# Second cross-attention's weight folds: two heads at once on 64-row halves of TensorE, folds regrouped

## The chip, the cores and the metric

One core of one Trainium2 chip runs the whole computation, two sequences of 512 tokens with 128 features. The metric is the device time of one execution in microseconds: 346.1 us before the change, the median of three runs (345.12, 346.10 and 346.39). A profile is of one more execution.

## The reference, cut to what matters

Two layers, each a cross-attention over 154 context tokens and a feed-forward part. The change is about the second cross-attention (16 heads of 64):

```python
x = x + xattn0(layernorm(x), ctx)          # 8 heads of 4
x = x + self_attention(layernorm(x))       # 16 heads of 8, causal, rotary, conv before
x = x + moe(layernorm(x))                  # 4 experts
q = layernorm(x) @ Wq                      # second cross-attention, 16 heads of 64
k, v = split(ctx @ Wkv)
dots = einsum('bhnd,bhmd->bhnm', q, k) * 64 ** -0.5 - (1 - mask) * 1e6
x = x + einsum('bhnm,bhmd->bhnd', softmax(dots), v) @ Wout + bout
x = x + ffn1(x)                            # small units, one Win and one Wout
```

The context and the weights are known from the start. So the kernel folds them: for each head h it computes `kk[h] = Wq[h] @ k[h]^T` (128 features x 154 keys) and `vw[h] = v[h] @ Wout[h]` (154 keys x 128 features), and the attention itself is then `x @ kk[h]`, softmax, and a sum with `vw[h]`.

## The kernel before, in words

The program writes one instruction list per engine: `sp` (SyncE, which issues DMAs), `pool` (GpSimd), `dve` (VectorE), `act` (ScalarE) and `pe` (TensorE). Each engine works through its list in order. Everything between engines goes by semaphores: an instruction that waits holds up all that is behind it on its engine.

In time, the stages are: the first cross-attention (stage A, units of eight heads by 128 tokens), the self-attention of both sequences, the experts, the second cross-attention (stage C) and the last feed-forward part. The folds for stage C have nothing to wait for but their weights. They are laid into the gaps of earlier stages by a written list, `PREC`, of 50 jobs. Head pairs of one 128-column chunk c of the weights (c = 0 to 7) make a chunk:

- `k` c and `v` c: one full-height matmul each (context against a chunk of Wk or Wv), for two heads; 308 and 320 columns.
- `kk` h: one job per head, 308 columns. The two heads of a chunk lie in the two 64-row halves of `wqT`, so each head's keys are held in `kz` with zeros in the other half, and a matmul runs over all 128 rows.
- `vw` (g, b): the four heads of two chunks against a Wout laid out with zeros (`woutZ`), two matmuls of 256 columns for the first 128 keys. `vr` (g, b): the same for the last 26 keys, four matmuls with 32 output partitions.
- `xv` b: not a fold; the values of sequence b of the self-attention, four matmuls.

TensorE issues a job in `fold_C`, ScalarE copies its result from PSUM to SBUF in `copy_C`, both in the order of the list. A float32 matmul stands in the trace as two passes, each with a weight load; so a `k` or `kk` job is two matmul records. The PSUM bank of job n is n mod 3 for n < 32, and after that bank 4 or 7. A job waits until the last job on its bank has been copied, and for the `k` or `v` job that it reads.

Where the list runs: jobs 0 to 2 and 3 to 5 inside the last units of stage A (`F_UNIT`). Then `queries_keys(0)` (the queries and keys of sequence 0, eight passes of 512 columns). Then jobs 6 to 25, up to `F_LN`. Then `turn("b")` transposes the normalised sequence 1; ScalarE copies it with scale and bias to `HT` (line 1150) and VectorE convolves it (lines 821 to 825). Then jobs 26 to 29, `queries_keys(1)`, and jobs 30 and 31. At `F_LATE` = 32 the first scores begin: 20 steps m of `scores_for_maximum`, whose row maxima VectorE takes (`maximum`, line 872). TensorE may be up to three steps ahead of VectorE, as there are three pairs of banks. From m = 2 on, one job of the list (32 to 49) follows each step. During these steps GpSimd splits the queries and keys of sequence 1 (lines 575 to 585), and SyncE stores them (lines 470 and 472) and, behind these, the maxima of chunk 0 (line 464). After step 19 come the score steps s of the self-attention, each with a ring of further maxima (line 882).

GpSimd zeroes `woutZ` (line 536) and `kz` (line 548) ahead of its stage-A units. SyncE's load of Wout waits for the first of them.

Of the kernel before, what the change touches and what calls it, by code (L numbers as in the profile page):

```python
# [27 lines left out]
P = 128  # L28
# [3 lines left out]
KEYS = 154  # L32
# [61 lines left out]
def program(nc, t_in, out):  # L94
    ctx = ExitStack()
    with ctx:
# [71 lines left out]

        cw = sb("cw", [P, 7632])
# [7 lines left out]
        assert c.at <= 7632  # L177
        c = Carve(cw)
# [68 lines left out]

        F_UNIT = (3, 6, 9)
        F_QKV = (14,30)
        F_LN = 26  # L250
        F_LATE = 32
        F_VALUES = 42
        F_MAX = 45

        def prec_jobs():

            for c in range(HC // 2 + 1):
                if c < HC // 2:
                    yield "k", c, 2
                    yield "v", c, 1  # L260
                if c >= 1:
                    yield "kk", 2 * c - 2, 1
                    yield "kk", 2 * c - 1, 1
                if c in (2, 4):
                    for b in range(B):
                        yield "vw", (c // 2 - 1, b), 1
                        yield "vr", (c // 2 - 1, b), 1
            for g in (2, 3):
                for b in range(B):
                    yield "vw", (g, b), 1  # L270
                    yield "vr", (g, b), 1


        PREC = list(prec_jobs())

        def fold_bank(n):
            if n < F_LATE:
                return n % 3
            return 7 if n % 2 else 4

        for b in range(B):
            PREC.insert(F_QKV[b], ("xv", b, 1))
        N_PREC = sum(j[2] for j in PREC)


        ld_x = [sem(f"ld_x{b}") for b in range(B)]
# [57 lines left out]
        PER = {"A": 1, "C": 2}  # L344
        LN_BANK = 7
        R_AT, R_COLS = 64, (QT + 1) * E
        Q4_BANK = (2, 7)
# [3 lines left out]
        SHIFTS = {"A": 2, "C": 3}  # L351
        Z_OWN, Z_CTX, Z_EARLY, Z_WOUT, Z_SLOT, Z_ALL = 1, 2, 5, 6, 8, 15 + SLOTS

# [36 lines left out]
        def first_bank(m):  # L390
            return (0, 2, 5)[(m - M0) % 3]

# [5 lines left out]
        def ring_bank(k):  # L398
            return 5 + k % 2

# [10 lines left out]
        def slot_bank(b, part):  # L411
            return 6 if part else LN_BANK

# [6 lines left out]
        def _(sp):  # L420
# [81 lines left out]
        def _(pool):  # L502
# [635 lines left out]
        def _(act):  # L1138
# [49 lines left out]
            def copy_C(n0, n1):  # L1188

                for n in range(n0, n1):  # L1190
                    kind, i, _ = PREC[n]
                    act.wait_ge(preC_mm, n + 1)
                    bank = fold_bank(n)
                    if kind == "k":
                        if n == 0:
                            act.wait_ge(zeroed, Z_ALL)
                        for j in range(2):
                            r = slice(64 * j, 64 * j + 64)
                            copy(kz[r, i % 2, j, :], PS[r, bank, 0:B * KEYS], float(HDC) ** -0.5).then_inc(preC_act, 1)
                    elif kind == "v":  # L1200
                        copy(vT[:, i % 4, :], PS[:, bank, 0:B * KPAD]).then_inc(preC_act, 1)
                    elif kind == "kk":
                        copy(kkC[:, :, i * KEYS:(i + 1) * KEYS],
                             PS[:, bank, 0:B * KEYS].rearrange("p (b k) -> p b k", b=B)).then_inc(preC_act, 1)
                    elif kind == "vw":
                        g, b = i
                        copy(vwCm[:, b, 512 * g:512 * g + 512], PS[:, bank, :]).then_inc(preC_act, 1)
# [43 lines left out]

            copy_C(F_LN, F_VALUES)
            act.wait_ge(preC_act, sum(j[2] for j in PREC[:F_VALUES]))
            values(0)
            no_values(0)
            copy_C(F_VALUES, F_MAX)
            copy_maxima(0)
# [118 lines left out]
        def _(pe):  # L1376
# [135 lines left out]
            def fold_C(n0, n1):  # L1512

                done = [0]
                for kind, i, k in PREC:
                    done.append(done[-1] + k)
                for n in range(n0, n1):
                    kind, i, _ = PREC[n]
                    bank = fold_bank(n)
                    if n == 0:  # L1520
                        pe.wait_ge(ld_c, 80)
                        pe.wait_ge(unit_shift["A"], SHIFTS["A"] * NT)
                    if n == F_LATE:
                        pe.wait_ge(ln_T["b"], B)
                        pe.wait_ge(qkv_read, 4 * B)
                    elif 3 <= n < F_LATE:
                        pe.wait_ge(preC_act, done[n - 2])
                    elif n >= F_LATE + 2:
                        pe.wait_ge(preC_act, done[n - 1])

                    if n == F_MAX:
                        pe.wait_ge(m_copied, 1)
                    if kind == "kk":
                        pe.wait_ge(preC_act, done[1 + PREC.index(("k", i // 2, 2))])
                    elif kind in ("vw", "vr"):
                        pe.wait_ge(preC_act, done[1 + PREC.index(("v", 2 * i[0] + 1, 1))])
                    if kind == "k":
# [3 lines left out]
                    elif kind == "kk":  # L1541
                        q = mm(PS[:, bank, 0:B * KEYS], wqT[:, i // 2, :], kz[:, (i // 2) % 2, i % 2, :])
                    elif kind == "vw":
                        g, b = i
                        for c in range(2):
                            q = mm(PS[:, bank, 256 * c:256 * c + 256], vT[:, (2 * g + c) % 4, b * KPAD:b * KPAD + KM],
                                   woutZ[:, 2 * g + c])
                    elif kind == "vr":
                        g, b = i
                        for j in range(4):  # L1550
                            c = 2 * g + j // 2
                            q = mm(PS[32 * j:32 * j + 32, bank, 0:D], vT[:, c % 4, b * KPAD + KM:b * KPAD + KPAD],
                                   woutZ[:, c, j % 2, :])
# [49 lines left out]
            fold_C(F_QKV[1], F_LATE)  # L1603
            pe.wait_ge(preC_act, sum(j[2] for j in PREC[:F_LATE]))
            pe.wait_ge(qkv_read, 4 * B)
            pe.wait_ge(consts_ready, 2)
            def turn_maxima(c):

                pe.wait_ge(m_part, 3 * (c + 1))
                if c == 0:  # L1610
                    pe.wait_ge(preC_act, sum(j[2] for j in PREC[:F_MAX - 1]))
                elif c == 1:
# [397 lines left out]
```

## Time and profile before

| | before |
|---|---|
| three runs, median (lowest, highest) | 346.1 us (345.12, 346.39) |
| the profiled execution: its own time | 344.6 us |
| its span, first to last instruction | 342.7 us |
| TensorE busy in the span | 319.4 us (93%) |
| VectorE, ScalarE, GpSimd busy | 240.8, 216.5, 127.6 us |
| TensorE's granted clock | 1.000 of full speed |
| chain that ended last: TensorE, ScalarE, VectorE | 64%, 13%, 12% |

The span lies 1.9 us under the execution's own time, and that is 1.5 us under the median of the three runs. Busy time of TensorE counts modelled matmul ends. "PEld" rows are its weight loads. A line number of TensorE or of a ScalarE copy is that of a helper (1378 is `mm`, 1140 is `copy`, 1393 and 1695 are transposes), so such rows are told apart by their tensors: `cw` is the buffer that holds the weights of the folds and their `k` and `v` results.

### The profile page before, as it was taken

To read this page: it belongs to the slowest core of one execution; us is meant where nothing else is said; L and a number is where in the kernel's file an instruction comes from. 1 tells how busy PE (TensorE), PEld (TensorE's weight loads), DVE (VectorE), ACT (ScalarE), POOL (GpSimd) and SP (SyncE) were. 2 spreads that over 40 slices of the span, in tenths; PEclk is the share of its full clock that TensorE was granted. 3 is DMA by queue.
4 is the path that set the end of the run, shared out by engine and by line. 5 is a ranking of instruction groups with operands and counts; after the bars stand their busy time and mean duration, and the time that the engine had idled before them with its cause. 6 is when DMAs were issued, how large, how long until landed. Compare 5 with 4: busy or idle time off the path is not lost.

```text
span 342.7 us, 6887 instructions
## 1 busy us (share of the span) xinstructions
PE 319.4 (93%) x2398; PEld 228.1 (67%) x2398; DVE 240.8 (70%) x594; ACT 216.5 (63%) x641; POOL 127.6 (37%) x183
## 2 busy tenths in 40 slices
PE   7799989998999999999899998998999899999886
PEld 2348878664655444455544898995678687878675
DVE  4988875884776788777652463369787867888476
ACT  1388885374455756555468754754766676676995
POOL 3455563110731444310631260410695525545400
PEclk9999999999999999999999999999999999999999
DMA  7590000084852430073002003200200000000002
GB/s 209 187 282 7 2 0 2 10 273 137 237 187 70 118 95 1 3 288 83 4 18 71 2 23 91 59 0 1 55 17 17 0 2 0 4 0 0 2 0 63
DMA packets 21880, 22.47 MB, mean 66 GB/s; under 512 B 3894, under 2 KB 18646, under 8 KB 21846
## 3 DMA queue, kind: packets, MB, share of 16 engines
q1 hardware_dynamic: 18982, 16.78, 16.8%
q10 hardware_dynamic: 2352, 4.20, 3.6%
q0 software_dynamic: 512, 1.05, 1.0%
q8 instruction: 20, 0.33, 0.4%
q14 instruction: 14, 0.11, 0.1%
HBM read 14.22 MB, written 7.60 MB: 64 GB/s over the span
## 4 chain that ended last, share of the span: by engine, by line
PE 64%; ACT 13%; DVE 12%; issue 4%; POOL 4%; DMA 3%; ACTq 0%; POOLq 0%; DVEq 0%
PE PS L1378 57%; PE PS L1432 5%; ACT big L1166 5%; ACT big L1354 3%; POOL big L528 2%; DVE big L690 2%; DVE big L715 2%; DMA X<-in_x 1%; PE PS L1695 1%; DMA XN<-scr_y,pos 1%; DVE mB L882 1%; DVE stats L656 1%; DVE XN L667 1%; ACT big L1140 1%; POOL big L530 1%
## 5 line engine op out<-in xcount | busy, mean ns | idle before, releaser
L1378 PE MATMUL PS<-big 128*128 128x128 f32 (+10 forms) x592 | 95.6, 308 | 6.6 <-DVE mB L882 2.3
L1378 PEld LDWEIGHTS PS<-big 128*128 128x128 f32 (+3 forms) x592 | 58.3, 150 | 34.7 <-issue 11.3
L528 POOL TENSOR_TENSOR big<-big,urec 128x1024 f32<-128x1024 f32 x24 | 45.6, 1898 | 59.9 <-DVE urec L722 45.5
L1166 ACT ACTIVATE big<-big 128x154 f32<-128x154 f32 x192 | 60.5, 318 | 10.1 <-DVE big L690 5.0
L1296 ACT ACTIVATE big<-PS 128x1024 f32<-128x1024 f32 (+3 forms) x64 | 42.9, 702 | 30.2 <-PE PS L1378 30.1
L1140 ACT ACTIVATE big<-PS 128x1280 f32<-128x1280 f32 (+2 forms) x30 | 32.3, 1087 | 27.0 <-PE PS L1432 24.5
L882 DVE TENSOR_REDUCE mB<-PS 128x2 f32<-128x256 f32 (+2 forms) x66 | 38.6, 600 | 11.9 <-PE PS L1378 11.6
L1378 PE MATMUL PS<-kkC,XT 128*128 128x462 f32 (+1 forms) x96 | 36.0, 511 | 1.9 <-DVE big L715 1.9
L1378 PE MATMUL PS<-cstb 128*128 128x128 bf16 x192 | 37.5, 220 | 0.0
L516 POOL TENSOR_TENSOR rstd<-ve,minus_half 128x4 f32<-128x4 f32 (+2 forms) x13 | 13.2, 1016 | 63.4 <-DVE ve L662 63.4
L1166 ACT ACTIVATION_READ_ACCUMULATOR big<-big 128x1 f32 x192 | 36.1, 188 | 0.0
L1378 PEld LDWEIGHTS PS<-vwCm,big 128*128 128x128 f32 x256 | 30.9, 192 | 3.9 <-ACT big L1140 1.3
L1432 PE MATMUL PS<-cst,big 128*128 128x128 f32 x240 | 30.6, 275 | 2.4 <-POOL big L530 1.8
L1378 PE MATMUL PS<-vwCm,big 128*128 128x128 f32 x256 | 31.3, 276 | 1.0 <-DVE X L745 0.5
L704 DVE TENSOR_REDUCE mraw<-PS 128x3 f32<-128x462 f32 (+1 forms) x48 | 26.0, 579 | 7.2 <-PE PS L1378 5.8
L1432 PEld LDWEIGHTS PS<-cst,big 128*128 128x128 f32 x240 | 26.6, 141 | 6.4 <-POOL big L530 6.2
L715 DVE SCALAR_TENSOR_TENSOR big<-PS,rowbias,umax 128x462 f32<-128x462 f32 (+1 forms) x48 | 27.5, 629 | 0.0
L1378 PEld LDWEIGHTS PS<-kkC,XT 128*128 128x128 f32 x96 | 17.0, 190 | 15.0 <-issue 11.9
L1378 PE MATMUL PS<-big,cw 128*32 128x512 f32 (+3 forms) x256 | 23.8, 444 | 0.3
L1378 PE MATMUL PS<-cw 128*32 128x128 f32 (+2 forms) x128 | 22.5, 351 | 0.8 <-ACT vwCm L1140 0.7
L606 POOL TENSOR_SCALAR_AFFINE_SELECT big<-big 128x256 f32<-128x256 f32 x32 | 12.9, 408 | 24.2 <-ACT big L1296 23.9
L1378 PEld LDWEIGHTS PS<-cstb 128*128 128x128 bf16 x192 | 18.9, 98 | 3.2 <-issue 1.6
(191 smaller groups left out, 508.1 us busy)
## 6 DMA issues: line engine op xcount, KB each, us to landing
scr_qk<-big SPq DMA_DIRECT2D x12, 384.0 KB, 3.4
big<-scr_qk SPq DMA_DIRECT2D x16, 288.0 KB
big<-in_wv ACTq DMA_DIRECT2D x1, 2048.0 KB, 7.9
scr_x<-zrow SPq DMA_DIRECT2D x2, 448.0 KB, 7.0
scr_y<-big SPq DMA_DIRECT2D x2, 448.0 KB, 3.9
X<-in_x ACTq DMA_DIRECT2D x2, 256.0 KB, 4.0
big<-in_A_WoT ACTq DMA_DIRECT2D x1, 512.0 KB, 5.0
cw<-in_C_Wk SPq DMA_DIRECT2D x1, 512.0 KB, 4.7
```

The lines of the kernel that those rows point to most:

```text
L516: pool.tensor_tensor(rstd[:, s], ve[:, s], minus_half[:, s], ALU.pow).then_inc(ln_rstd[name], 1)
L528: pool.tensor_tensor(pn[:, 0:GH * P].rearrange("p (h k) -> p h k", h=GH), Pt[u % 3][:, :, 0:KM], r.to_broadcast([P, GH, KM]), ALU.mult).th ...
L606: pool.affine_select(PTb[:, slot:slot + 2, 0:P], PTb[:, slot:slot + 2, 0:P], [[0, 2], [1, P]], ALU.is_ge, 0.0, base=0, channel_multiplier= ...
L704: own(dve.tensor_reduce(mraw[:, u % 2, h0:h1], s, AX.X, ALU.max))
L715: dve.scalar_tensor_tensor(Pt[u % 3][:, h0:h1, :], s, bias(u), umax[:, u % 2, h0:h1].unsqueeze(2).to_broadcast([P, h1 - h0, KEYS]), ALU.ad ...
L882: dve.tensor_reduce(mB[:, b, h:h + len(heads), qt], PS[:, ring_bank(k), 0:len(heads) * w].rearrange("p (j w) -> p j w", w=w), AX.X, ALU.ma ...
L1140: return act.activation(dst, src, ACT.Copy, scale=scale)
L1166: i = act.activation(Pt[u % 3][:, h, :], Pt[u % 3][:, h, :], ACT.Exp, accum_out=usum[:, u % 3, h:h + 1])
L1296: act.activation(PTb[:, slot:slot + 2, 0:w], PS[:, 2 * pair:2 * pair + 2, 0:w], ACT.Exp, scale=float(HDB) ** -0.5).then_inc(st_exp, 1)
L1354: act.activation(RJ[:, j, c], sT[:, c], ACT.Relu, scale=vec[:, V_W1 + j:V_W1 + j + 1], bias=vec[:, V_B1 + j:V_B1 + j + 1]).then_inc(relu_r ...
L1378: return pe.matmul(o, lhsT, rhs, start=start, stop=stop)
L1432: i = pe.transpose(PS[:, T_BANK[st] + k // 4, (k % 4) * P:(k % 4) * P + P], PN[v % 2][:, k * P:k * P + P], ident)
```

## The change

The two heads of a chunk are multiplied as two matmuls of 64 rows each, one on rows 0 to 63 and one on rows 64 to 127, each into a bank of its own. `kz` and `woutZ` with their zeros and memsets are gone, `kT` and `wout` are plain. A `kk` job now covers two heads and a `vw` job writes two banks, and each is copied by one ScalarE instruction over both banks (616 columns for `kk`, 512 for `vw`). A `k` result is copied whole, in one instruction in place of two of 64 partitions. The list has 42 jobs. `fold_banks` gives each job one or two neighbouring banks, of 0 to 2 before `F_LATE` and of 6 and 7 after it, and the copy that it has to wait for.

The new places: jobs 0 to 2 and 3, 4 in stage A; 5 to 26 between `queries_keys(0)` and `turn("b")`; 27 to 32 before `queries_keys(1)`; 33 after it. Jobs 34 to 41 (four `vw`, four `vr`) follow the even steps m = 2 to 16. The maxima of chunk 0 are turned at m = 13.

The list with its banks, and behind the slash the job whose copy a job waits for:
`k0[0] v0[1] k1[2] | v1[0]/k0 kk0[1,2]/k1 | k2[0]/v1 v2[1]/kk0 kk1[0,1]/v2 vw00[0,1]/kk1 vr00[2] xv0[0]/vw00 vw01[1,2]/vr00 vr01[0]/xv0 k3[1]/vw01 v3[2]/vw01 kk2[0,1]/k3 k4[2]/v3 v4[0]/kk2 kk3[1,2]/k4 vw10[0,1]/kk3 vr10[2]/kk3 vw11[0,1]/vw10 vr11[2]/vr10 k5[0]/vw11 v5[1]/vw11 kk4[0,1]/v5 k6[2] | v6[0]/kk4 kk5[1,2]/k6 k7[0]/v6 v7[1]/kk5 kk6[0,1]/v7 kk7[0,1]/kk6 | xv1[2]/k7`; then in the score steps `vw20[6,7] vr20[6]/vw20 vw21[6,7]/vr20 vr21[6]/vw21` and the same for 30 and 31.

```diff
-        woutZ = c.f32(HC * D).rearrange("p (c j o) -> p c j o", c=8, j=2)
-        kz = c.f32(2 * 2 * B * KEYS).rearrange("p (r j n) -> p r j n", r=2, j=2)
+        wout = c.f32(HC * D // 2).rearrange("p (c o) -> p c o", c=8)
+        kT = c.f32(2 * B * KEYS).rearrange("p (r n) -> p r n", r=2)
...
-        F_UNIT = (3, 6, 9)
-        F_QKV = (14,30)
-        F_LN = 26
-        F_LATE = 32
-        F_VALUES = 42
-        F_MAX = 45
+        F_UNIT = (3, 5)
+        F_QKV = (10, 33)
+        F_LN = 27
+        F_LATE = 34
+        F_MAX = 40
+        M_FOLDS = range(2, 18, 2)
+        M_CHUNK0 = 13
...
+        def fold_banks():
+            used, at = {}, 0
+            for n, (kind, _) in enumerate(PREC):
+                ring = (0, 1, 2) if n < F_LATE else (6, 7)
+                if n == F_LATE:
+                    at = 0
+                pair = kind in ("kk", "vw")
+                if pair and at % len(ring) == len(ring) - 1:
+                    at += 1
+                banks = [ring[(at + j) % len(ring)] for j in range(1 + pair)]
+                at += len(banks)
+                FOLD_BANKS.append(banks)
+                FOLD_AFTER.append(max(used.get(k, 0) for k in banks))
+                for k in banks:
+                    used[k] = n + 1
...
-        AV_BANK = 4
-        GROUP_BANK = ((7, 7, 7, 7), (6, 5, 6, 5))
+        AV_BANK = 6
+        GROUP_BANK = ((7, 7, 7, 7), (4, 5, 4, 5))
...
-            sp.wait_ge(zeroed, Z_WOUT)
-            for j in range(2):
-                sp.dma_start(woutZ[64 * j:64 * j + 64, :, j, :],
-                             i["C_Wout"].rearrange("(c j e) o -> j e c o", j=2, e=HDC)[j]).then_inc(ld_c, 16)
+            sp.dma_start(wout, i["C_Wout"].rearrange("(c p) o -> p c o", p=P)).then_inc(ld_c, 16)
...
-            pool.memset(woutZ, 0.0).then_inc(zeroed, 1)
-            pool.memset(kz, 0.0).then_inc(zeroed, 1)
...
                     if kind == "k":
-                        for j in range(2):
-                            r = slice(64 * j, 64 * j + 64)
-                            copy(kz[r, i % 2, j, :], PS[r, bank, 0:B * KEYS], float(HDC) ** -0.5).then_inc(preC_act, 1)
+                        copy(kT[:, i % 2, :], PS[:, bank, 0:B * KEYS], float(HDC) ** -0.5).then_inc(preC_act, 1)
...
                     elif kind == "kk":
-                        copy(kkC[:, :, i * KEYS:(i + 1) * KEYS],
-                             PS[:, bank, 0:B * KEYS].rearrange("p (b k) -> p b k", b=B)).then_inc(preC_act, 1)
+                        copy(kkC[:, :, 2 * i * KEYS:(2 * i + 2) * KEYS].rearrange("p b (j k) -> p j b k", j=2),
+                             fold_out(n, B * KEYS).rearrange("p j (b k) -> p j b k", b=B)).then_inc(preC_act, 1)
...
+                    after = FOLD_AFTER[n]
                     if kind == "kk":
-                        pe.wait_ge(preC_act, done[1 + PREC.index(("k", i // 2, 2))])
+                        after = max(after, 1 + PREC.index(("k", i)))
...
+                    if after:
+                        pe.wait_ge(preC_act, after)
...
                     elif kind == "kk":
-                        q = mm(PS[:, bank, 0:B * KEYS], wqT[:, i // 2, :], kz[:, (i // 2) % 2, i % 2, :])
+                        for j, half in enumerate(HALVES):
+                            q = mm(PS[:, FOLD_BANKS[n][j], 0:B * KEYS], wqT[half, i, :], kT[half, i % 2, :])
                     elif kind == "vw":
                         g, b = i
                         for c in range(2):
-                            q = mm(PS[:, bank, 256 * c:256 * c + 256], vT[:, (2 * g + c) % 4, b * KPAD:b * KPAD + KM],
-                                   woutZ[:, 2 * g + c])
+                            for j, half in enumerate(HALVES):
+                                q = mm(PS[:, FOLD_BANKS[n][j], c * D:c * D + D],
+                                       vT[half, (2 * g + c) % 4, b * KPAD:b * KPAD + KM], wout[half, 2 * g + c, :])
...
-                if m >= 2 and late < len(PREC):
+                if m in M_FOLDS:
                     fold_C(late, late + 1)
                     late += 1
-                if late == F_MAX:
+                if m == M_CHUNK0:
                     turn_maxima(0)
```

The four matmuls of `vr` change in the same way: two heads of a chunk on the two halves, each with 32 output partitions, all in one bank. The banks of the first scores and of the ring move from 5, 6 to 4, 5.

## Rows read from the trace of the kernel before

**Rows 1.** Stretches of the trace: length, busy time (count) by engine, clock, DMA.

```profile
core 0: us, PE busy (x) PEld busy (x) DVE busy (x) ACT busy (x) POOL busy (x), PEclk, DMA share, GB/s
8.00:12.00 4.00, 2.44 (x10) 0.98 (x9) 3.80 (x17) 1.02 (x2) 0.98 (x1) 1.00 0.87 313
62.00:88.00 26.00, 24.60 (x124) 14.72 (x123) 17.46 (x43) 12.88 (x31) 2.66 (x3) 1.00 0.52 157
88.00:109.00 21.00, 20.19 (x151) 12.68 (x149) 15.62 (x20) 10.64 (x24) 9.63 (x13) 1.00 0.56 173
```

**Rows 2.** Chain that ended last, in order: start, length, engine, tensor, line.

```profile
58.77 20.05 PE PS L1378 x106
...
87.88 10.68 PE PS L1378 x68
...
109.41 4.35 PE PS L1378 x31
```

**Rows 3.** Timeline, 25 to 88 us: start, length, engine, instruction, count, idle before.

```profile
25.83 0.80 PE L1378 MATMUL PS<-big 32*128 32x308 f32 x8 [0.61 <-DVE big L690]
...
66.57 1.33 ACT L1140 ACTIVATE cw<-PS 64x308 f32<-64x308 f32 x3 [5.76 <-PE PS L1378]
...
70.48 0.16 PEld L1378 LDWEIGHTS PS<-cw 128*32 128x32 f32 x8 [0.33 <-issue]
...
79.52 1.32 PE L1378 MATMUL PS<-ctxT,cw 128*128 128x308 f32 x4
...
80.34 1.33 ACT L1140 ACTIVATE cw<-PS 64x308 f32<-64x308 f32 x3
...
80.68 0.68 PE L1378 MATMUL PS<-cw 128*128 128x308 f32 x2
...
86.88 0.60 ACT L1140 ACTIVATE XN<-PS 128x512 f32<-128x512 f32 x1 [4.88 <-PE PS L1378]
...
87.40 0.43 ACT L1140 ACTIVATE kkC<-PS 128x308 f32<-128x308 f32 x1
```

**Rows 4.** Timeline, 69 to 71 us, as rows 3.

```profile
69.42 0.73 PEld L1378 LDWEIGHTS PS<-cw 128*128 128x128 f32 x4 [0.20 <-issue]
...
70.59 0.60 ACT L1140 ACTIVATE vwCm<-PS 128x512 f32<-128x512 f32 x1 [0.65 <-PE PS L1378]
...
70.84 1.16 PE L1378 MATMUL PS<-aqkv,HC 128*128 128x128 f32 x8
```

**Rows 5.** Timeline, 76 to 88 us: from sequence 1's norm to the first scores.

```profile
76.31 1.12 DVE L667 TENSOR_SCALAR XN<-U,mv,rstd 128x128 f32<-128x128 f32 x4 [1.19 <-POOL rstd L516]
...
78.42 0.58 PEld L1393 LDWEIGHTS PS<-cst,XN 128*128 128x128 f32 x4
...
79.33 0.77 ACT L1150 ACTIVATE HT<-PS,vec 128x512 f32<-128x512 f32 x1
...
81.44 0.75 DVE L825 SCALAR_TENSOR_TENSOR HC<-HT,vec,HC 128x512 f32<-128x512 f32 x1
...
82.25 0.30 PEld L1378 LDWEIGHTS PS<-HC,aqkv 128*128 128x128 f32 x2 [1.37 <-DVE HC L825]
...
87.88 0.10 PEld L1378 LDWEIGHTS PS<-big 72*128 72x128 bf16 x1 [1.00 <-ACT kkC L1140]
```

**Rows 6.** Groups of instructions by line: busy, mean ns, idle before and its releaser.

```profile
L872 DVE TENSOR_REDUCE mB<-PS 128x2 f32<-128x256 f32 (+3 forms) x20 | 16.0, 824 | 6.1 <-PE PS L1378 6.1
```

**Rows 7.** Timeline, 88 to 106 us: VectorE's first maxima, GpSimd and SyncE.

```profile
88.32 3.47 DVE L872 TENSOR_REDUCE mB<-PS 128x2 f32<-128x256 f32 x5 [1.05 <-PE PS L1378]
...
96.42 2.13 POOL L585 TENSOR_TENSOR big<-big 128x1024 bf16<-128x1024 f32 x1
...
98.98 1.45 SPq L472 DMA_DIRECT2D scr_qk<-big  x1
...
103.61 1.85 SPq L464 DMA_DIRECT2D big<-nm  x3
```

**Rows 8.** Timeline, 19 us: GpSimd's first unit of stage A.

```profile
19.73 1.90 POOL L528 TENSOR_TENSOR big<-big,urec 128x1024 f32<-128x1024 f32 x1 [2.01 <-DVE urec L674]
```

More of the change, by code:

```diff
@@ L258, in prec_jobs, with fold_out @@
                 if c < HC // 2:
-                    yield "k", c, 2
-                    yield "v", c, 1
+                    yield "k", c
+                    yield "v", c
                 if c >= 1:
-                    yield "kk", 2 * c - 2, 1
-                    yield "kk", 2 * c - 1, 1
+                    yield "kk", c - 1
                 if c in (2, 4):
                     for b in range(B):
-                        yield "vw", (c // 2 - 1, b), 1
-                        yield "vr", (c // 2 - 1, b), 1
+                        yield "vw", (c // 2 - 1, b)
+                        yield "vr", (c // 2 - 1, b)
             for g in (2, 3):
                 for b in range(B):
-                    yield "vw", (g, b), 1
-                    yield "vr", (g, b), 1
+                    yield "vw", (g, b)
+                    yield "vr", (g, b)
         PREC = list(prec_jobs())
[L276 to L279, printed above, removed]
         for b in range(B):
-            PREC.insert(F_QKV[b], ("xv", b, 1))
-        N_PREC = sum(j[2] for j in PREC)
+            PREC.insert(F_QKV[b], ("xv", b))
+        N_PREC = len(PREC)
+        FOLD_BANKS, FOLD_AFTER = [], []
+        def fold_banks():
[13 more added lines that the diff above has]
+                    used[k] = n + 1
+        fold_banks()
+        def fold_out(n, cols):
+            lo = FOLD_BANKS[n][0]
+            return PS[:, lo:lo + 2, 0:cols]
         ld_x = [sem(f"ld_x{b}") for b in range(B)]
@@ L1190, in copy_C @@
                 for n in range(n0, n1):
[L1191 removed]
+                    kind, i = PREC[n]
                     act.wait_ge(preC_mm, n + 1)
[L1193 removed]
+                    bank = FOLD_BANKS[n][0]
                     if kind == "k":
[L1195 to L1199 removed]
+                        copy(kT[:, i % 2, :], PS[:, bank, 0:B * KEYS], float(HDC) ** -0.5).then_inc(preC_act, 1)
                     elif kind == "v":
@@ L1250, in copy_maxima @@
                 copy(nm3[:, c % 2], PS[0:3 * HG * QT, LN_BANK, M_AT:M_AT + P]).then_inc(m_copied, 1)
-            copy_C(F_LN, F_VALUES)
-            act.wait_ge(preC_act, sum(j[2] for j in PREC[:F_VALUES]))
+            copy_C(F_LN, F_LATE)
+            act.wait_ge(preC_act, F_LATE)
             values(0)
             no_values(0)
-            copy_C(F_VALUES, F_MAX)
+            copy_C(F_LATE, F_MAX)
             copy_maxima(0)
@@ L1512, in fold_C @@
             def fold_C(n0, n1):
-                done = [0]
-                for kind, i, k in PREC:
-                    done.append(done[-1] + k)
                 for n in range(n0, n1):
-                    kind, i, _ = PREC[n]
-                    bank = fold_bank(n)
+                    kind, i = PREC[n]
+                    bank = FOLD_BANKS[n][0]
                     if n == 0:
-                        pe.wait_ge(ld_c, 80)
+                        pe.wait_ge(ld_c, 64)
                         pe.wait_ge(unit_shift["A"], SHIFTS["A"] * NT)
@@ L1545, in fold_C @@
                         for c in range(2):
-                            q = mm(PS[:, bank, 256 * c:256 * c + 256], vT[:, (2 * g + c) % 4, b * KPAD:b * KPAD + KM],
-                                   woutZ[:, 2 * g + c])
+                            for j, half in enumerate(HALVES):
+                                q = mm(PS[:, FOLD_BANKS[n][j], c * D:c * D + D],
+                                       vT[half, (2 * g + c) % 4, b * KPAD:b * KPAD + KM], wout[half, 2 * g + c, :])
                     elif kind == "vr":
                         g, b = i
[L1550 to L1553, printed above, removed]
+                        for c in range(2):
+                            for j, half in enumerate(HALVES):
+                                s = 32 * (2 * c + j)
+                                q = mm(PS[s:s + 32, bank, 0:D], vT[half, (2 * g + c) % 4, b * KPAD + KM:b * KPAD + KPAD],
+                                       wout[half, 2 * g + c, :])
                     else:
@@ L1603, in _ @@
             fold_C(F_QKV[1], F_LATE)
-            pe.wait_ge(preC_act, sum(j[2] for j in PREC[:F_LATE]))
+            pe.wait_ge(preC_act, F_LATE)
             pe.wait_ge(qkv_read, 4 * B)
@@ L1610, in turn_maxima @@
                 if c == 0:
-                    pe.wait_ge(preC_act, sum(j[2] for j in PREC[:F_MAX - 1]))
+                    pe.wait_ge(preC_act, F_MAX)
                 elif c == 1:
```

22 lines of the change are left out of this document (10 added, 12 removed).

## The prediction

> **What bounds the kernel now.** Start with the chain that ended last, and look for the engine that it stays on where the folds are. It runs on TensorE's matmuls from 58.8 us for 20 us, takes the norm and convolution of sequence 1 on the way, and is on TensorE again from 87.9 us, through the first scores [rows 2]. So both stretches that the change touches lie on the path. The stretches by busy time say how full: TensorE is busy 24.6 of 26.0 us before the first scores and 20.2 of 21.0 us in them, at a granted clock of 1.00 [rows 1]. Busy there counts the modelled ends, so it does not say whether passes follow each other; the timeline does. In the score steps VectorE has 16.0 us of maxima and waits 6.1 us for TensorE, 1.05 us of that ahead of the first [rows 6, 7]. The reader should see two different limits: in the score steps TensorE's work alone, before them a ring of three banks in which TensorE and ScalarE take turns.
>
> **Prices.** A `k` and a `v` job are four passes in 1.32 us [rows 3]; less some 0.27 us for a cold start and the last one's end, that is 1.05 us, 0.53 us a job. A `kk` job is two passes in 0.68 us, 0.53 us of TensorE too. From the first pass of a job that starts cold to its first copy it is 80.34 - 79.52 = 0.82 us [rows 3]. From the end of a copy (87.40 + 0.43) to the load that it releases it is 0.05 us [rows 3, 5]. So a job of 308 columns that waits for a copy costs 0.87 us until its own copy can start, whatever ScalarE does meanwhile.
>
> Copies: 308 columns 0.43 us, 512 columns 0.60 us [rows 3], so 0.00083 us a column more; the two-bank `kk` copy of 616 columns is 0.43 + 308 x 0.00083 = 0.69 us (bounds 0.60 and two single ones, 0.86). `k` was two half copies: three copies in 1.33 us, 0.44 each [rows 3]; it is one now.
>
> Two heads at once: the trace has no 64-row pair. The nearest row has four matmuls of 32 rows, 308 columns, each in its bank: eight passes in 0.80 us, where one full-height job takes 0.68 us [rows 3]. I take a pair to cost as one job, 0.87 us with its release; the bound above is no overlap, 0.53 us more, and below 0.05 us less. A `vw` pair: four passes of 256 columns took 70.59 - 69.42 = 1.17 us from load to copy. Eight passes of 128 columns took 1.16 us, less 0.37 us of start and end 0.11 us a step [rows 4]. Four steps of 128 in place of 256 save 0.44 us: 0.73 us, 0.78 with the release. I take 0.85 us, as two halves load weights at once; bounds 0.78 and, without overlap, 1.25 us.
>
> A change of tile shape: the load of a 32-column job comes 0.33 us after the load before, and the load after one 0.20 us, both released by nothing [rows 3, 4]. The engine runs empty first. I take 0.1 us going in and 0.2 us coming out where no copy wait covers it. The Trainium skill (TensorEngine Tiling (Array Packing), "Key Properties") says that changing the tiling mode drains TensorE; the trace agrees, 0.33 and 0.20 us. By that rule `kk` and `vw` now pay too, and the sum has it.
>
> **What goes at no cost.** The two memsets and the wait of Wout's load: GpSimd sits idle 2.0 us before its first unit, which VectorE releases [rows 8]. Taken away, that wait gets longer, nothing moves. Nor does SyncE's earlier load; the first fold that reads it comes far later. In stage A TensorE saves about 0.1 us; I leave it out. The banks moved from 5, 6 to 4, 5 keep three pairs and a ring of two: nothing.
>
> **Folds before the first scores.** A pair needs two of three banks, so where two pairs follow each other, or a pair follows its neighbour, nothing can be issued until the copy is done. I walk the list by the ends of copies. The `v2` copy ends at 67.4 (before: 66.57 + 1.33 = 67.9, one half copy more [rows 3]).
>
> - kk1 waits for v2: 0.87 + 0.69 = 1.56. vw00 on the same banks: 0.85 + 0.60 = 1.45. xv0 waits for it: 0.05 + 1.16 + 0.04 + 0.60 = 1.85 [rows 3, 4]. vw01's passes follow those of xv0: 0.7.
> - k3 waits for vw01: 0.87 + 0.44 = 1.31; v3 right behind, 0.54; kk2's passes follow, 1.0. v4 waits for kk2: 1.31. kk3 behind: 1.0.
> - vw10 on kk3's banks 1.45, vw11 on vw10's 1.45, k5 1.31, v5 0.54, kk4 waits for v5 1.56. k6's passes lie beside kk4's copy.
>
> Together 17.0 us: kk4 is copied at 84.4, and the turn of sequence 1 starts at 84.2. Before, it loads at 78.4, with its data ready at 77.4 [rows 5]. ScalarE's copies in it are only five k, four v, four kk, four vw, four vr and xv, 10.8 us; the rest is nine exposed releases.
>
> The turn's passes take 0.6 us, ScalarE's `HT` copy 0.77, the convolution 81.44 + 0.75 - 80.10 = 2.1 us [rows 5]: ready at 87.7. But six jobs now stand before `queries_keys(1)`, against three, and their copies come after `HT`: v6 copied at 85.9, kk5 86.8, k7 87.2, v7 (waits for kk5) 88.1, kk6 (waits for v7) 89.65, kk7 waits for kk6 on the same banks. Its passes and the way out of the mode take 0.8 us, so `queries_keys(1)` loads at 90.45. Before, it was 82.25, waiting for the convolution [rows 5]: +8.2 us. Behind it `kk9` is gone: the scores start after xv1's copy, 87.48 + 0.05 - 82.25 = 5.28 us later, against 87.88 - 82.25 = 5.63 [rows 3, 5]. First scores at 95.7: **+7.8 us** (bounds +7.2 with no drains, +12.6 with no overlap of halves).
>
> **Score steps.** Ten jobs of 0.53 us have left (5.3), four vw are halved (1.7), and drains add about 1.2: TensorE needs 20.2 - 5.8 = 14.4 us, less than VectorE's 16.0. VectorE sets the pace: 0.44 us until its first maximum, 16.0, and I take 0.6 for the first steps and for folds that wait for ScalarE's value copies. That is 17.05 us, against 0.44 + 16.0 + 5.05 = 21.5 before: **-4.45 us** (bounds -5.05, no wait left, and -3.5). What is late next is chunk 0's maxima: GpSimd's last split ends as late as before after the scores' start, SyncE issues its stores behind [rows 7], and they land some 15.5 us after the start, which is before 17.05 but not by much.
>
> **The sum.** +7.8 - 4.45 = +3.35 us. What follows step 19 depends on nothing older, so the shift stays. The profiled execution's 344.6 us (span 342.7) becomes 348.0; on the median of the runs, 1.5 us above it, 346.1 + 3.4 = **349.5 us**.
>
> **Rivals.**
> - The halves don't overlap, the change doesn't do what it says. Seven kk pairs cost 0.53 more, the vw 0.4 each, on the path: +4.9 us, 354.4. Against it is the row of four quarter-height matmuls.
> - Faster: the releases are hidden and ScalarE's copies alone set the pace. The 10.8 us of copies end at 77.2, the turn starts about when its data is ready, at 77.6. Then HT and 3.4 us of copies, `queries_keys(1)` at 82.3, the scores at 87.6, and only the 4.45 us gained remain, with 0.3 more: 341.4. Twelve releases are exposed (nine and three); it decides when one costs 0.28 us less than 0.85, that is under 0.57. For it speaks that ScalarE has 12.9 of 26 us in this stretch; against it that 0.82 us stands in the timeline each time.
> - The clock falls, as TensorE waits more: passes at 1.2 GHz over some 20 us add about 4 us, 353.5. Against it, the stretch of 8 to 12 us with 2.4 of 4.0 us busy has 1.00 [rows 1].
> - Between: releases partly hidden, 346.
>
> The Trainium skill's same page ("PSUM Bottleneck") says that tiling speeds up TensorE but not the evacuation of PSUM, which may then be the limit. That speaks against this change in the fold stretch; the trace agrees that a single job's passes (0.53 us) already match its copy (0.43 us).
>
> **How the numbers follow.** Forecast 0.61 (its own range 348 to 351.5), no overlap 0.10, clock 0.07, faster 0.14, between 0.08. Range 346 to 354.5: the top takes in the second case, the bottom the weaker half of the first. About 0.5% is what a measurement of this kernel tells from no change, 1.7 us. Slower by more: 0.61 + 0.10 + 0.07 + 0.01 = 0.79; same 0.07; faster 0.14.
>
> **What would show it.** The turn of sequence 1 near 84 us and waiting for no data; `queries_keys(1)` near 90.5, released by a fold and not by the convolution; about nine gaps of 0.7 to 0.8 us between ScalarE's copies before the turn. A kk pair with four passes that end within 0.8 us. The 20 maxima in 17 us, with VectorE idle under 1.5 us. A turn before 80 us would make the prediction wrong, whatever the score steps do.

## The result: 1.1% slower, as forecast, and the profile after

The kernel after takes 349.87 us (median of 4 runs, 348.99 to 350.58), the kernel before 346.23 in the same comparison (345.12 to 346.39): a ratio of 1.0114, with a 95% interval of 1.0087 to 1.0141. The profiled execution took 349.33 us with a span of 347.6, against 344.6 and 342.7. All ratios here compare fast runs alone: a run more than 1.5% above the fastest of its kernel is left out, which happens to three of ten in kernel 1 and three of four in kernel 5.

Now the stretches that the prediction spoke of. The first timeline of the kernel after covers 66.5 to 70 us, the first pairs, read like [rows 3].

```profile
66.10 0.97 ACT L1156 ACTIVATE cw<-PS 128x308 f32<-128x308 f32 x2 [5.69 <-PE PS L1391]
...
67.12 0.79 PE L1391 MATMUL PS<-cw 64*128 64x308 f32 x4 [0.53 <-ACT cw L1156]
67.96 0.68 ACT L1156 ACTIVATE kkC<-PS 128x616 f32<-128x616 f32 x1 [0.89 <-PE PS L1391]
...
68.69 0.80 PEld L1391 LDWEIGHTS PS<-cw 64*128 64x128 f32 x16 [1.27 <-ACT kkC L1156]
...
69.46 0.60 ACT L1156 ACTIVATE vwCm<-PS 128x512 f32<-128x512 f32 x1 [0.81 <-PE PS L1391]
```

Four passes of 308 columns take 0.79 us in the 64-row shape, where two full-height ones took 0.68 [rows 3]: the halves overlap. Then TensorE and ScalarE alternate: the copy at 67.96 starts 0.84 us after the pair's first load, the next pair's load waits for that copy's end, and the copy at 69.46 comes 0.82 us after the copy before it ended (67.96 + 0.68 = 68.64).

The same view from the last copies before the turn of sequence 1 to the first maximum, the counterpart of [rows 5]:

```profile
81.44 0.97 ACT L1156 ACTIVATE cw<-PS 128x308 f32<-128x308 f32 x2 [0.71 <-PE PS L1391]
83.30 0.68 ACT L1156 ACTIVATE kkC<-PS 128x616 f32<-128x616 f32 x1 [0.89 <-PE PS L1391]
...
83.55 0.62 PEld L1406 LDWEIGHTS PS<-cst,XN 128*128 128x128 f32 x4
...
84.45 0.78 ACT L1166 ACTIVATE HT<-PS,vec 128x512 f32<-128x512 f32 x1
...
89.36 0.79 PE L1391 MATMUL PS<-cw 64*128 64x308 f32 x4 [0.78 <-ACT kkC L1156]
90.07 0.30 PEld L1391 LDWEIGHTS PS<-HC,aqkv 128*128 128x128 f32 x2 [0.42 <-issue]
...
95.35 0.09 PEld L1391 LDWEIGHTS PS<-big 72*128 72x128 bf16 x1 [0.88 <-ACT XN L1156]
...
95.80 1.90 DVE L888 TENSOR_REDUCE mB<-PS 128x2 f32<-128x256 f32 x3 [0.69 <-PE PS L1391]
```

The turn loads at 83.55 us, 5.1 later than before, and is released by nothing: it stands behind the folds. `queries_keys(1)` loads at 90.07, right behind a pair's passes, where before it waited for the convolution [rows 5]. The first scores come at 95.36, 7.5 us later than before, and the first maximum at 95.80 (88.32).

The score steps, by the group of VectorE's maxima (as [rows 6]) and one stretch from the first scores to the ring's first:

```profile
L888 DVE TENSOR_REDUCE mB<-PS 128x2 f32<-128x256 f32 (+3 forms) x20 | 15.1, 818 | 1.6 <-PE PS L1391 1.6
```

```profile
core 0: us, PE busy (x) PEld busy (x) DVE busy (x) ACT busy (x) POOL busy (x), PEclk, DMA share, GB/s
95.36:111.81 16.45, 14.34 (x147) 8.42 (x147) 15.10 (x20) 6.75 (x13) 10.11 (x13) 1.00 0.51 168
```

VectorE waits 1.6 us in all, 0.69 of it ahead of the first, against 6.1. So it still waits 0.9 us between its maxima, while their busy time falls from 16.0 [rows 6] to 15.1 us: the mean of one is about the same (818 and 824 ns), but where they follow each other without a wait their spans overlap a little. The twenty maxima end 15.96 us after the first began (111.76 - 95.80); before, 21.03 us (109.35 - 88.32). So 7.48 us late at the first maximum has become 2.41 us late at the last.

From there to the end the kernel after loses another 2.9 us in two places, of which 0.4 is won back. The windows show what the two places have in common (the last column but two is the granted clock):

```profile
108.00:112.00 4.00, 2.54 (x25) 1.17 (x18) 3.76 (x5) 1.30 (x2) 0.99 (x5) 1.00 0.58 173
112.00:114.00 2.00, 2.00 (x17) 0.99 (x15) 1.40 (x3) 1.17 (x2) 0.48 (x2) 0.97 0.36 92
114.00:118.00 4.00, 4.00 (x22) 1.34 (x21) 2.11 (x6) 1.64 (x4) 1.00 (x3) 0.59 0.03 7
118.00:122.00 4.00, 3.89 (x42) 1.88 (x38) 3.12 (x8) 3.04 (x6) 1.95 (x7) 1.00 0.65 178
164.00:168.00 4.00, 2.33 (x24) 1.20 (x23) 3.86 (x14) 2.61 (x4) 1.39 (x1) 1.00 0.00 0
168.00:172.00 4.00, 4.00 (x21) 1.36 (x20) 2.17 (x5) 0.81 (x1) 3.13 (x4) 0.57 0.02 3
```

Twice TensorE works 2.3 to 2.5 us of 4 while VectorE catches up, and right behind it the clock stands at 1.2 GHz, from 113.90 to 117.31 and from 168.51 to 171.93 us, 3.41 us each. The same instructions of VectorE, matched in the two traces, are 2.42 us late before the first fall and 3.98 behind it, 5.33 behind the second: +1.55 and +1.35 us. By 261 us it is 4.92, and the span ends 4.9 us later.

The second of the two waits is no work of the change. The profiled run of the kernel before has it too, and its clock stays up:

```profile
160.00:164.00 4.00, 2.33 (x24) 1.21 (x23) 3.86 (x14) 2.63 (x4) 1.39 (x1) 1.00 0.00 0
164.00:168.00 4.00, 3.97 (x38) 1.99 (x36) 2.65 (x5) 1.50 (x3) 3.65 (x7) 1.00 0.03 5
```

The first wait is longer by the change: TensorE stands still 1.10 us ahead of the ring's first scores, against 0.43 us before.

### The profile page after: what moved, and what is told of

Its sections match the earlier page's. It is cut to its first block, busy times and chain, and to the rows that moved or that the text cites. A ratio compares the mean times of both kernels' runs of the same rounds, so it can differ in the third digit from the quotient of the medians.

```text
span 347.6 us, 6900 instructions
## 1 busy us (share of the span) xinstructions
PE 319.0 (92%) x2430; PEld 223.4 (64%) x2430; DVE 239.8 (69%) x594; ACT 212.8 (61%) x625; POOL 125.2 (36%) x181
## 4 chain that ended last, share of the span: by engine, by line
PE 63%; ACT 13%; DVE 13%; issue 4%; POOL 3%; DMA 2%; ACTq 0%; POOLq 0%; DVEq 0%
PE PS L1391 56%; PE PS L1445 5%; ACT big L1182 4%; ACT big L1367 3%; POOL big L546 2%; DVE mB L888 2%; DVE big L706 2%; DVE big L731 1%; DMA X<-in_x 1%; PE PS L1706 1%; DVE mB L898 1%; DVE stats L672 1%; DVE XN L683 1%; ACT kkC L1156 1%; ACT big L1156 1%
## 5 line engine op out<-in xcount | busy, mean ns | idle before, releaser
L1391 PEld LDWEIGHTS PS<-big 128*128 128x128 f32 (+3 forms) x592 | 58.4, 151 | 39.4 <-issue 14.5
L546 POOL TENSOR_TENSOR big<-big,urec 128x1024 f32<-128x1024 f32 x24 | 45.6, 1899 | 62.6 <-DVE urec L738 45.5
L898 DVE TENSOR_REDUCE mB<-PS 128x2 f32<-128x256 f32 (+2 forms) x66 | 38.6, 599 | 14.8 <-PE PS L1391 14.4
L1391 PEld LDWEIGHTS PS<-kkC,XT 128*128 128x128 f32 x96 | 17.0, 190 | 14.5 <-issue 11.7
L1391 PE MATMUL PS<-big,cw 128*32 128x512 f32 (+3 forms) x256 | 25.6, 473 | 0.2
L1391 PE MATMUL PS<-cw 64*128 64x128 f32 (+2 forms) x160 | 15.2, 326 | 4.3 <-ACT kkC L1156 2.3
```

What stands on the lines that cost most here:

```text
L546: pool.tensor_tensor(pn[:, 0:GH * P].rearrange("p (h k) -> p h k", h=GH), Pt[u % 3][:, :, 0:KM], r.to_broadcast([P, GH, KM]), ALU.mult).th ...
L898: dve.tensor_reduce(mB[:, b, h:h + len(heads), qt], PS[:, ring_bank(k), 0:len(heads) * w].rearrange("p (j w) -> p j w", w=w), AX.X, ALU.ma ...
L1391: return pe.matmul(o, lhsT, rhs, start=start, stop=stop)
```

## The experiments

Eight kernels ran, on two chips, each beside runs of the kernel before on the same chip: 345.58 us median on the first (kernels 1, 2, 3 and 5), 348.42 on the second (4, 6, 7 and 8). So compare ratios, not times. The kernel after is not among them; its 1.0114 is from its own comparison with 346.23 us. Between 184 and 204 us, at a clock of 1.00, the instructions in the second chip's traces fall back some 1.6 us that those in the first chip's don't, so how late an instruction comes is compared only up to the last of the twenty maxima. The expectations call kernel 1 a_six, kernel 3 a_clock and kernel 7 best.

**1. Six banks for the pairs.** Banks 3 to 5 lie idle between the two `queries_keys`.

```diff
-                ring = (0, 1, 2) if n < F_LATE else (6, 7)
-                if n == F_LATE:
+                ring = (6, 7) if n >= F_LATE else (0, 1, 2, 3, 4, 5) if F_UNIT[1] <= n < F_QKV[1] else (0, 1, 2)
+                if n in (F_UNIT[1], F_QKV[1], F_LATE):
...
+                    if n < F_QKV[1] and FOLD_BANKS[n][-1] > 2:
+                        pe.wait_ge(qkv_read, 4)
```

> The changed kernel with one edit: jobs 5 to 32 take their banks from a ring of six (0 to 5) in place of three; banks 3 to 5 are idle between the rotation of sequence 0 and queries_keys(1). Same matmuls, same copies, same order. Theory (a pair on two of three banks makes TensorE wait for each copy): the turn of sequence 1 moves from 83.8 us to about 79, queries_keys(1) from 90.1 to about 84.2, the first scores from 95.4 to 89.5, the score steps stay 16.4 us; 5.5 us less, about 344.3 us. Rival (the folds' passes or ScalarE's copies themselves are too much for this place): under 1.5 us less, and ScalarE's gaps stay.

Measured: 344.36 us, median of ten, ratio 0.9954 (0.9922 to 0.9986). Three of the ten runs had a mean clock of 0.96 and took 352 us. ScalarE's copies in the stretch whose counterpart above had gaps of 0.71 and 0.89:

```profile
76.91 0.97 ACT L1156 ACTIVATE cw<-PS 128x308 f32<-128x308 f32 x2 [0.29 <-PE PS L1391]
78.17 0.69 ACT L1156 ACTIVATE kkC<-PS 128x616 f32<-128x616 f32 x1 [0.29 <-PE PS L1391]
78.88 0.43 ACT L1156 ACTIVATE cw<-PS 128x308 f32<-128x308 f32 x1
```

The turn loads at 78.42 us, 5.1 earlier than after and where it was in the kernel before (79 was expected), the first scores come at 89.21 (89.5). The last of the twenty maxima ends at 105.61, 6.2 earlier than after. The clock falls for 6.8 us, from 105.46 to 112.28, and again at 163.49, which takes much of it back:

```profile
104.00:106.00 2.00, 0.88 (x6) 0.39 (x7) 1.61 (x2) 1.02 (x1) 0.32 (x1) 0.86 0.71 205
106.00:112.00 6.00, 6.00 (x28) 2.35 (x26) 3.34 (x7) 2.80 (x4) 1.31 (x4) 0.50 0.13 33
```

So the releases on three banks are what the change pays before the turn: same matmuls, same copies, same order, and the 5.1 us are gone.

**2. No overlap of the halves.** Both heads of a `kk` pair on the first half's rows, so that the second can't run beside the first.

```diff
-                            q = mm(PS[:, FOLD_BANKS[n][j], 0:B * KEYS], wqT[half, i, :], kT[half, i % 2, :])
+                            q = mm(PS[:, FOLD_BANKS[n][j], 0:B * KEYS], wqT[HALVES[0], i, :], kT[HALVES[0], i % 2, :])
```

> The changed kernel, with both matmuls of a kk job on rows 0 to 63 (the second head of each chunk is computed from the first one's half, so the output differs): two matmuls of the same size and count that can't lie side by side. Theory (the halves overlap, a pair costs as much as one job): a pair's four passes take 1.3 us in place of 0.79, seven pairs stand on the path before the first scores, 3.6 us more, about 353.5 us. Rival (what a pair saves isn't overlap, or the halves hardly overlap): within 0.5 us of the changed kernel.

Measured: 355.76 us, ratio 1.0328 (1.0257 to 1.04). The first pair:

```profile
67.39 1.30 PE L1391 MATMUL PS<-cw 64*128 64x308 f32 x4 [0.53 <-ACT cw L1156]
...
68.72 0.68 ACT L1156 ACTIVATE kkC<-PS 128x616 f32<-128x616 f32 x1 [1.39 <-PE PS L1391]
```

1.30 us in place of 0.79, and a release of 1.39 in place of 0.89: +0.50 a pair. The first maximum comes at 99.60, 3.80 us later than after. Of that, 0.26 us is there before the seven pairs (62.40 against 62.14 us at the same instruction of VectorE), which leaves 0.51 a pair. The rest of the 5.2 us in the span is a clock that falls for 6.8 us at 115.89 where after had 3.4. The ratio lies 2.1% over that of the kernel after, some 7 us and twice the forecast; its runs had mean clocks of 0.975 to 0.985, those of after 0.985 to 0.990. So the time is a poor measure here, but the passes settle it: the halves do run side by side in the kernel after, and the rival "no overlap" is refuted.

**3. Work for the clock before the ring.** Five products that nobody reads, on bank 7, in TensorE's wait ahead of the ring.

```diff
+                if k == 0:
+                    pe.wait_ge(preC_act, N_PREC)
+                    hold_clock(LN_BANK, 5)
                 if k < 2:
                     pe.wait_ge(s_max, M0)
```

> The changed kernel with five matmuls of constants into bank 7 between the first score step's first pair and the ring's first scores, where TensorE waits 1.1 us for VectorE's last maximum. Theory (the granted clock falls to 0.50 at 113.9 us for 3.4 us because TensorE has waited in 108 to 112 us): the fall at 113.9 is gone, the one at 168.5 stays, 1.5 us less, about 348.4 us. Rival (the fall has nothing to do with this wait, it comes in any kernel): both falls stay, 0 to 0.2 us more.

Measured: 347.6 us, ratio 1.0074 (1.0044 to 1.0104), against 1.0114 for after. The products lie in the gap, and the ring's first scores still come 1.5 us behind the last step's:

```profile
109.69 0.38 PE L1391 MATMUL PS<-big 75*128 75x512 bf16 x1
109.91 1.24 PE L1391 MATMUL PS<-onesb 128*128 128x512 bf16 x5
111.18 0.23 PE L1391 MATMUL PS<-big 72*128 72x128 bf16 x1
```

No fall follows in the profiled run; the one at 167.14 to 170.55 stays. Seven of the ten runs have a mean clock of 0.994 or 0.995, as the profiled run with its one fall, and three have 0.989 or 0.990, as the profiled run of after with two; the four runs of after had 0.985 to 0.990. The time is 0.8 us under the forecast, but the interval of the ratio overlaps that of after, so it is the clocks that show the effect. On its own chip the kernel is 2.0 us over before.

**4. The same products in both places.** As 3, and behind the maxima turned in ring step 20:

```diff
                     turn_maxima(S_CHUNK.index(s))
+                    if s == 20:
+                        for _ in range(6):
+                            mm(PS[:, LN_BANK, 0:M_AT].rearrange("p (a n) -> p a n", a=3), onesb[:],
+                               onesb[:].unsqueeze(1).to_broadcast([P, 3, P]))
```

> The kernel after, unchanged but for the same products in both places. a_clock, with the first five alone, took the fall at 113.9 away and left one at 167.14 to 170.55. Theory: with the six as well no fall is left, and the time is another 1.35 us lower, 346.2 us, which is 0.2 % over before: what the folds cost without the clock, +7.5 us before the first scores, less 5.05 us in the score steps and 0.5 us in the stage before. Rival (the second fall comes whatever TensorE does there): 347.6 us as a_clock.

Measured: ratio 1.0013 (0.9991 to 1.0035), 348.84 us against 348.42. In the profiled run the clock is 1.00 to the end; the first line is kernel 3's at the second place, the second this kernel's:

```profile
164.00:172.00 8.00, 6.26 (x41) 2.96 (x40) 4.37 (x10) 3.09 (x6) 5.35 (x9) 0.79 0.02 4
```

```profile
164.00:172.00 8.00, 7.22 (x60) 4.18 (x59) 4.97 (x15) 3.35 (x6) 5.35 (x9) 1.00 0.02 4
```

The ratio is what was expected (0.2% over before), the clock only half of it: six of its twelve runs had a mean clock of 1.000 and took 348.13 us (median), the other six 0.995 and 349.64, so a fall still comes in every other run, and one costs 1.5 us. The kernel before has such falls too. Its runs on the first chip, by mean clock: 344.59 us at 1.000 (6 runs), 345.62 at 0.993 to 0.995 (9), 347.17 at 0.988 to 0.990 (4); on the second 346.62 (1), 348.08 (13) and 349.35 (9). So it ran without a fall less often on the second chip, which lowers the ratios there a little. At a clock of 0.995 this kernel is 349.64 - 348.08 = 1.6 us behind before. That is the price of the change without the clock; its trace has +2.2 us at the last of the twenty maxima. The expectation takes the 0.5 us of stage A off a second time: the +7.5 us are counted from the span's start and hold it already, so its own terms give 7.5 - 5.05, about +2.4 us.

**5. Folds moved into the score steps.** Fewer jobs before the first scores, ten more among the steps on the late ring of two banks.

```diff
-        F_QKV = (10, 33)
-        F_LN = 27
-        F_LATE = 34
-        F_MAX = 40
-        M_FOLDS = range(2, 18, 2)
+        F_QKV = (10, 23)
+        F_LN = 19
+        F_LATE = 24
+        F_MAX = 36
+        M_FOLDS = range(2, 20)
...
-            act.wait_ge(preC_act, F_LATE)
+            F_VALUES = 1 + PREC.index(("v", 7))
+            copy_C(F_LATE, F_VALUES)
+            act.wait_ge(preC_act, F_VALUES)
             values(0)
             no_values(0)
-            copy_C(F_LATE, F_MAX)
+            copy_C(F_VALUES, F_MAX)
```

> The changed kernel with its matmuls and its rings of three and two banks, but ten more jobs in the score steps, one after each step from m = 2: turn of sequence 1 after job 18, queries_keys(1) after job 22, first scores after job 23. Theory (before the scores each pair costs exposed waits, in the score steps only TensorE's passes beyond VectorE's 16 us): turn at 77.1 us when its data is ready, first scores at 86.0 in place of 95.4, the score steps 24.1 us in place of 16.4; together 1.7 us less, about 348.2. Rival (regrouping is what pays, folds in score steps are dear): 2 us or more slower than the changed kernel.

Measured: 354.26 us median of 4, no ratio, since three of the four had a clock of 0.957 to 0.966. The fourth, at 0.989, took 348.82 us, which is 0.9% over before. The expectation is neither met nor refuted by that one run: it can't be told from after's 1.1%. The profiled run is one of the three. A first fall of the clock, from 69.85 to 73.26 us, lies ahead of its turn, which loads at 77.79, and the first maximum starts at 87.13 us. The twenty maxima then take 30.45 us (117.58 - 87.13). Three stretches, the first two and the last of those at the low clock:

```profile
98.00:101.00 3.00, 1.75 (x10) 0.88 (x12) 2.02 (x2) 2.52 (x4) 0.54 (x1) 0.93 0.51 173
101.00:105.00 4.00, 3.76 (x28) 1.93 (x26) 0.66 (x2) 1.28 (x2) 0.00 (x0) 0.50 0.20 67
105.00:120.00 15.00, 14.51 (x95) 7.37 (x87) 6.46 (x9) 5.01 (x10) 1.24 (x5) 0.50 0.15 40
```

TensorE waits 1.25 us for the copy of a pair that holds both late banks, up to 100.57 us, where the clock falls; it stays at 1.2 GHz for 23.9 us, and TensorE, busy 14.5 of 15 us there, is the bound. Whether the wait brought the fall on is not shown. Nor does any trace show how long the twenty maxima take in this kernel at full clock.

**6. Six banks for the single jobs.** The kernel before, its jobs 6 to the second `queries_keys` on six banks.

```diff
-                return n % 3
+                return n % 6 if F_UNIT[1] <= n < F_QKV[1] else n % 3
...
-                        pe.wait_ge(preC_act, done[n - 2])
+                        same = [p for p in range(n) if fold_bank(p) == bank]
+                        if same:
+                            pe.wait_ge(preC_act, done[same[-1] + 1])
+                        if bank > 2:
+                            pe.wait_ge(qkv_read, 4)
```

> The kernel before (single jobs, 128 rows with zeros), its jobs 6 to the second queries_keys on six banks in turn in place of three, nothing else. It tells apart what six banks give by themselves from what they give to the pairs. Theory (a single job on three banks already has two others behind it, its release hides but for some): turn at about 77.3 us (78.42 before), first maximum about 1 us earlier, 345 us against 346, where the six banks gave the paired kernel 5 us at the turn. Rival (releases cost the single jobs as much as the pairs, so the whole gain of a_six was the banks and the pairs give nothing): turn at 75 or earlier and 342 us or less.

Measured: 347.62 us, ratio 0.9971 (0.995 to 0.9993). The turn loads at 77.28 us (78.42 in before), the first maximum starts at 87.18 (88.32), and the maxima take the same 21.03 us. So the banks are worth 1.1 us at most to single jobs at the turn, and 5.1 us to pairs. Of the 1.1 us, 0.7 is there at 62.6 us already (61.90 against 62.61 at the same instruction of VectorE), before any job uses the new banks; of the 5.1 it is 0.2 (61.91 in kernel 1 against 62.14 in after).

This tells less against the rival than it seems. The rival asked for a turn at 75 us, but the turn reads sequence 1's norm, which is ready at 77.4 us in before (76.31 + 1.12 [rows 5]) and at 76.7 here: no number of banks brings it to 75. And six banks leave the score steps as long as they were; what shortens them in the kernel after is that ten jobs have left them and that the four `vw` are halved. Single jobs in the new places were not run. An estimate from the rows: ten jobs of 0.53 us are 5.3 us more of TensorE work before the first scores, where it is busy 24.6 of 26 us [rows 1], for at most the 5.05 us that VectorE waits.

**7. Six banks and the jobs placed for them.** As 1, with:

```diff
-        F_QKV = (10, 33)
-        F_LN = 27
-        F_LATE = 34
-        F_MAX = 40
-        M_FOLDS = range(2, 18, 2)
+        F_QKV = (12, 31)
+        F_LN = 25
+        F_LATE = 33
+        F_MAX = 39
+        M_FOLDS = range(2, 20, 2)
...
-                ring = (6, 7) if n >= F_LATE else (0, 1, 2, 3, 4, 5) if F_UNIT[1] <= n < F_QKV[1] else (0, 1, 2)
+                ring = (6, 7) if n >= F_LATE else (0, 1, 2, 3, 4, 5) if F_UNIT[1] <= n < 29 else (0, 1, 2)
```

> The kernel after, with the first 24 fold jobs on six banks in turn, and the jobs put elsewhere: two more kk jobs before queries_keys(0) (F_QKV 10 to 12), two jobs more after queries_keys(1) (33 to 31), and one more fold among the score steps. Theory (the pairs cost time only because with three banks each holds two, so that every job stands behind a release; their halves do overlap, and the shorter score steps are real): turn at about 77.5 us (83.55 after), first maximum at about 87.8 (95.80), last maximum of the first twenty steps at about 104.5 (111.76, and 109.35 before), so 5 us ahead of the kernel before at that point. With a fall of the clock like those of the runs so far (1.4 to 3 us for each 3.4 or 6.8 us at 1.2 GHz, two of them) 343 to 344.5 us; with none 340.5. Rival (the 64-row pairs are slow in themselves): turn not before 80, first maximum not before 90, and 347 us or more.

Measured: 341.59 us (341.38 to 342.54), ratio 0.9803 (0.9772 to 0.9835). Turn 76.82, first maximum 87.91, last of the twenty 103.58: 5.8 us ahead of before and 0.9 ahead of what was expected. One fall of the clock is left, 3.41 us at 159.76, where two were expected. All six runs have a mean clock of 0.994 or 0.995. The time is under the 343 to 344.5 us expected, though this chip is the slower one. The group of the maxima:

```profile
L888 DVE TENSOR_REDUCE mB<-PS 128x2 f32<-128x256 f32 (+3 forms) x20 | 15.1, 820 | 2.1 <-PE PS L1391 2.1
```

**8. Kernel 7 with the products of 4.**

> As best, with matrix products that nobody reads where TensorE waits: five of 512 columns before the ring's first scores (after the wait for the last fold's copy) and six of 384 columns behind the maxima turned in step 20. Theory (both falls of the clock follow on the two stretches in which TensorE waits for VectorE, and the folds' shape only makes the first stretch longer): no fall at 104 to 112 and none at 163 to 172, and 1.4 us less for each: about 340.5 to 341 us. Rival (the falls come from elsewhere): the same as best.

Measured: 339.98 us (339.59 to 340.25), ratio 0.9751 (0.9721 to 0.9781), mean clock 0.999 or more in all six runs, and in the profiled one no fall before the last microsecond. The 1.6 us against kernel 7 is the price of its one fall. It is the fastest kernel of the study, 2.5% under before. Part of that is the clock and not the folds: the one run of before with a mean clock of 0.999 on this chip took 346.62 us, and against it the gain is 1.9%. The kernel before with such products in its waits was not run.

## Why the prediction was right

The forecast was 349.5 us and the time 349.87; the sum was +3.35 and the medians differ by 3.64. Point by point:

- **Folds before the first scores: +7.8, measured +7.5** (first scores 87.88 to 95.36; by matched instructions +7.83 at the rotary products of sequence 1, +7.48 at the first maximum). The +7.5 is counted from the span's start; at 62.6 us, ahead of this stretch, the kernel after was 0.47 us early, so the stretch itself cost 7.95. Every station came within 0.7 us: turn 84.2 forecast, 83.55 measured; `queries_keys(1)` 90.45 and 90.07, released by a fold; first scores 95.7 and 95.36. Of the gaps between ScalarE's copies before the turn there are eight of 0.65 to 1.08 us, for nine forecast. Kernel 1 confirms the cause: more banks, and 5.1 us at the turn are gone.
- **A pair costs as one job: 0.87 us forecast**; 0.89 measured ahead of a `kk` copy, 0.81 ahead of `vw`, a `kk` copy 0.68 for 0.69 and a pair's passes 0.79. The last pass of a pair (82.84 us) and the full-height pass behind it (83.19) start 0.35 us apart, where full-height passes of this size in a row start 0.26 apart: the way out of the shape costs 0.09 us there, for 0.2 forecast. The forecast had read 0.20 us from a load that comes 0.20 us after the one before it, which is no sign of a drain by itself: the loads of `queries_keys(1)`, all of one shape, stand 0.24 us apart. Kernel 2 shows what the rival would have cost.
- **Score steps: -4.45, measured -5.07** (21.03 to 15.96 us). The term was mis-sized by 0.6 us, and its parts by more: the forecast had 16.0 us of maxima and 0.6 of waits, the trace has 15.1 and 0.9. So the total lies at the bound of -5.05 "no wait left" although waits are left; VectorE's wait of 1.6 us in all misses the sign "under 1.5". TensorE's need came out as forecast, 14.4 and 14.34 us.
- **Stage A, left out as some 0.1 us, was -0.5 in the trace** (by matched instructions -0.27 at 6.4 us, ahead of the change's first fold, and -0.47 at 62.6). That is not shown to be the change: at 62.6 us kernel 3, with the same stage A, is 1.09 us ahead of before, and kernel 6, whose stage A is that of before, 0.7.
- **The clock, costed at nothing, was +2.9 us in the trace**, of which 0.4 is won back by 261 us. This is the step that failed: "against it, the stretch of 8 to 12 us with 2.4 of 4.0 us busy has 1.00". Behind a stretch almost as empty, 108 to 112 us with 2.54 of 4, the clock did fall. One row at 1.00 doesn't clear a wait, since one kernel's runs differ in it: the kernel before, with the same waits each time, had six runs of nineteen at 1.000 on the first chip and thirteen below. The rival had the mechanism and missed its size, two falls of 3.4 us and not 20 us (no row gave the 20 us or their 4 us), and its place, behind the score steps where TensorE had become the one that waits.

That the sum is within 0.3 us is luck. The trace has 7.5 - 5.1, which is +2.4 at the last of the twenty maxima, and the clock brought the span's difference to +4.9. The medians differ by less than the spans, by 3.64, because the profiled run of before was one at clock 1.000, 1.6 us under its median, as runs on the first chip at 1.000 and 0.995 differ by 1.0; the profiled run of after, 0.5 under its median, had two falls.

Of the rivals, "faster: the releases are hidden" fails at the gaps in ScalarE's row, and kernel 1 shows what it would have looked like; "no overlap" at kernel 2.

## What to carry to other kernels

Two heads at once take TensorE 0.79 us where two full-height jobs take 1.32, but a pair takes its banks two at a time: count how many results can be in flight before counting passes. The same edit lost 1.1% on three banks and, with the three idle ones and the jobs placed anew, won 2.0%; how much of that gain single jobs in the same places would have is not shown. Where an engine stops being the bound, look at its clock in the stretch behind the wait; a little work in the wait can be cheaper than the fall (1.6 us in kernel 8). And count a shift either from the span's start or from the start of the stretch, not from both.

## What the hardware showed that was not expected

- The clock's falls to 1.2 GHz lasted 3.41 us each in after, 6.83 us at the first one of kernels 1 and 2 and the only one of kernel 6, and 23.89 us at the second one of kernel 5. A fall of 3.4 us cost 1.35 to 1.55 us of the span.
- A fall comes in some runs of a kernel and not in others: kernel 4's twelve runs split six to six, 1.5 us apart, and the kernel before has three such levels on either chip. Much of what looks like noise in these times is the number of falls. What decides in which run a wait is followed by a fall stays open.
- A pair of 64-row matmuls of 308 columns ends 0.11 us later than a full-height one (0.79 against 0.68 us for all passes); on one half the two take 1.30. On two halves the passes start 0.01 us apart, on one half 0.26 us.
